# Transposes of the next expert group's rows, moved in front of the values products of their step

## The reference

```
xn  = layernorm(x)
out = x + attention(xn) + experts(xn)
attention: 16 heads of 8, causal softmax(q k^T / sqrt(8)) v, then w_proj and its bias
experts:   logits = xn Wg^T; the best 2 of 8 experts per token, gates = softmax of the two logits
           y = sum of gate * (gelu(xn W1 + b1) W2 + b2), inner size 512
```

## Time and profile before

| what | value |
|---|---|
| median of three runs (lowest, highest) | 749.66 us (740.96, 753.08) |
| the profiled execution's own time | 743.79 us |
| its span, first to last instruction | 742.0 us |
| TensorE busy, share of the span | 88% |
| VectorE, ScalarE, GpSimd busy | 71%, 59%, 37% |
| mean granted TensorE clock, share of full | 0.906 |

### The profile page before, as it was taken

How to read it: one execution, slowest core, us unless ns; L and a number is a source line. 1 busy time by engine, 2 the same in 40 slices (tenths; PEclk the granted TensorE clock), 3 DMA queues, 4 the chain that set the end, 5 groups by cost and what they waited for, 6 DMA issues and landing times.

```text
span 742.0 us, 14386 instructions
## 1 busy us (share of the span) xinstructions
PE 651.6 (88%) x4889; PEld 384.0 (52%) x4889; DVE 525.3 (71%) x1787; ACT 439.8 (59%) x652; POOL 275.2 (37%) x438
## 2 busy tenths in 40 slices
PE   5798977789893888999999999899999998999987
PEld 5554443344441546555565556556565556565533
DVE  6676677978883557668667766767777767767776
ACT  5025644536371567667576846767676757677654
POOL 5813530156776023342314322332414322333411
PEclk9556887979895799999999989999999999999979
DMA  6655572025311557144443507135443626220084
GB/s 162 196 110 158 142 200 33 20 74 192 98 58 52 161 178 192 46 123 142 128 135 97 178 19 193 61 97 172 126 139 102 175 77 186 82 83 15 29 211 129
DMA packets 95569, 88.45 MB, mean 119 GB/s; under 512 B 8560, under 2 KB 82984, under 8 KB 95496
## 3 DMA queue, kind: packets, MB, share of 16 engines
q1 hardware_dynamic: 90600, 77.21, 38.0%
q0 software_dynamic: 4544, 9.35, 3.8%
q10 hardware_dynamic: 352, 0.97, 0.5%
HBM read 49.79 MB, written 21.32 MB: 96 GB/s over the span
## 4 chain that ended last, share of the span: by engine, by line
PE 69%; DVE 15%; ACT 6%; issue 4%; DMA 3%; POOL 2%; ACTq 0%; DVEq 0%
PE ov L912 19%; PE aux L875 15%; PE aux L973 10%; DVE junk L1112 6%; PE aux L925 5%; PE sc L829 3%; PE sc L895 3%; PE aux L930 3%; ACT probs L780 2%; PE sc L830 2%; PE sc L831 2%; DVE maxes L1110 2%; POOL xs L688 2%; PE aux L953 2%; DMA qT<-mT 1%
## 5 line engine op out<-in xcount | busy, mean ns | idle before, releaser
L780 ACT ACTIVATE probs<-sc 128x1024 f32<-128x1024 f32 (+1 forms) x320 | 286.6, 941 | 168.9 <-PE sc L895 167.6
L1112 DVE CUSTOM_DVE_ANT_0 junk<-aux,cst 128x512 bf16<-128x512 f32 (+3 forms) x512 | 219.9, 487 | 39.7 <-PE aux L875 36.5
L875 PE MATMUL aux<-kT,qT 32*128 32x512 f32 (+3 forms) x768 | 201.0, 448 | 42.9 <-DVE maxes L1112 13.2
L696 POOL TENSOR_SCALAR_AFFINE_SELECT probs<-probs 128x256 f32<-128x256 f32 x224 | 89.1, 411 | 293.8 <-ACT probs L780 288.6
L1110 DVE TENSOR_REDUCE maxes<-aux 128x1 f32<-128x512 f32 x256 | 163.2, 683 | 20.6 <-PE aux L875 17.4
L912 PE MATMUL ov<-probs,v 128*32 128x512 f32 (+3 forms) x1536 | 171.1, 535 | 0.9 <-POOL probs L696 0.5
L875 PEld LDWEIGHTS aux<-kT,qT 32*128 32x128 f32 x768 | 91.2, 199 | 126.1 <-DVE maxes L1112 36.1
L895 PE MATMUL sc<-qT,kT 32*128 32x512 f32 (+3 forms) x768 | 140.7, 425 | 7.5 <-DMA qT<-mT 5.3
L711 POOL DMA_INDIRECT ys<-ysb,back x78 | 75.8, 972 | 99.7 <-DVE ysb L1160 53.9
L973 PEld LDWEIGHTS aux<-w2all,hid 128*128 128x128 f32 x624 | 77.5, 195 | 40.7 <-DVE maxes L1110 25.1
L973 PE MATMUL aux<-w2all,hid 128*128 128x128 f32 x624 | 90.0, 288 | 0.3 <-DVE kql L1049 0.3
(11 more groups left out here) (121 smaller groups left out, 582.0 us busy)
## 6 DMA issues: line engine op xcount, KB each, us to landing
w1b<-w_scr SPq DMA_DIRECT2D x39, 512.0 KB, 4.4
w2all<-in_L_ffn_W SPq DMA_DIRECT2D x39, 256.0 KB, 3.7
xs<-ysb SPq DMA_DIRECT2D x13, 387.0 KB, 5.9
kT<-kqh SPq DMA_DIRECT2D x32, 128.0 KB, 2.8
w_scr<-w1b SPq DMA_DIRECT2D x8, 512.0 KB, 4.1
qT<-kqh SPq DMA_DIRECT2D x30, 128.0 KB, 2.9
xrow<-in_L_attn_x SPq DMA_DIRECT2D x7, 512.0 KB, 5.8
xsin<-xs SPq DMA_DIRECT2D x6, 516.0 KB
```

Source lines behind the costliest of these rows:

```text
L696: last_ = nc.gpsimd.affine_select(out=block_, in_=block_, compare_op=ALU.is_ge, fill=0.0, base=0, pattern=[[0, 2], [1, P]], channel_multip ...
L780: nc.scalar.activation(probs[:, s % 2, 2 * half:2 * half + 2, 0:cols], pair(part)[:, :, 0:cols], ACT.Exp).then_inc(sc_done, 1)
L875: last_ = nc.tensor.matmul(bank(part)[:, at:at + cols], qT[n % 3][rows, P * i:P * i + P], kT[n % 3][rows, k0:k0 + cols], start=True, stop= ...
L1112: last_ = nc.vector.tensor_tensor_reduce(out=junk[:, AUXI[part] % 3, at:at + cols], in0=src, in1=cmask[:, W - cols:W], scale=1.0, scalar=L ...
```

## The change

Both `rows_in` parts of a unit, at steps 8 and 9, are appended to the list before the `values` part of the same step; before, they were appended near its end, behind `values`, the late `rows`, `send`, `down` and `load_down`. It concerns the 20 `rows_in` of units 4 to 13 (groups 1 to 10); those of group 0 stay. No instruction is added or removed.

```
--- before.py
+++ after.py
@@ -223,6 +223,8 @@
         parts.extend(x for x in group if x not in only[:4])
         if s == 0 and not f:
             late_values()
+        if nf and s in (8, 9):
+            parts.append(("rows_in", nf, s - 8))
         if s > 0:
             parts.append(("values", n, s - 1))
         parts.extend(due)
@@ -262,8 +264,6 @@
             parts.append(("load_down", f + 1))
         if nf is not None and s == (6 if nf else 8):
             parts.append(("load_rows", nf))
-        if nf and s in (8, 9):
-            parts.append(("rows_in", nf, s - 8))
```

## The result

The changed kernel takes 742.86 us (median of 22 runs, 734.78 to 752.35); the kernel before, run beside it 22 times, 746.69 us (738.04 to 754.25). The ratio is 0.9949, 95% interval 0.9928 to 0.9971: 0.5% faster, about 3.8 us (2.2 to 5.4), and far inside 2%. Over all 22 the means are 743.57 and 746.19 us, 2.6 us apart, give or take 2.5 (95%). Of the 5.4 us between forecast and measurement, 3.0 are the level: the median of before was 749.66 over three runs and is 746.69 over twenty-two.

The account below looks back on a forecast made before the run. TensorE was taken as the bound, with 69% of the chain that ended last. Six units gaining 0.34 us and four losing 0.17 gave 1.4 us, so 749.66 - 1.4 = 748.3 us; 8-in-10 range 741 to 754.

Parts of the forecast that it names:

- ScalarE's order limits the gain: Step 8, units with a `down`: two exponentials precede the cast, so 0.74 us of the transposes' 2 us move arrives.
- Unit 5, half 0: Units with a `down` in step 8, first `rows_in`: TensorE takes step 9's second adjacent `max` 0.53 us earlier.
- Half 1: Step 9's transposes newly wait for the opening `max`'s bank: 0.19 us with a `down` in step 8, 0.17 without.
- only reordered: TensorE's pieces from the released `max` to the next unit's `max`, 3.21 or 3.43 us, were taken as merely reordered.
- the net of unit 5: Each of six units with a `down` in step 8: 0.53 - 0.19 = 0.34 us gained.
- Unit 6: Each of four units without a `down` in step 8: released `max` unmoved, new bank wait in step 9 loses 0.17 us.
- Sum: All ten changed units: 6 x 0.34 - 4 x 0.17 = 1.4 us gained.
- the whole stall: Rival, step 9: TensorE's whole wait for the low part goes, 9.7 us gained, 740.0 us; chance 0.10.
- all units behave like unit 6: Rival: in all ten units only the step 9 bank wait is left, 1.7 us lost, 751.4 us; chance 0.17.
- The rows were there: Rival denied here: earlier transposes wait for the row load, 759.7 us less what is won; chance 0.03.
- The clock did not fall: Rival denied here: TensorE's clock falls once in each of ten units, 17 us less 1.4, 765.3 us; chance 0.04.
- the Trainium skill's rule on PSUM-queue cycling: Brief TensorE idling while cycling through PSUM banks lets the clock oscillate; one fall costs about 1.7 us, making a loss.

Follow-up runs that it names:

- e4_half0_between: Against the kernel before: the step 8 `rows_in` put ahead of the second scores of step 8, the step 9 one left in place; ratio 0.9965 to the kernel before.
- e1_half0_only: Against the changed kernel: only the step 8 `rows_in` stays in front of `values`, the step 9 one returns to its step's end; 0.9952 to the kernel before, 758.02 us.
- e2_half1_only: Against the changed kernel: only the step 9 `rows_in` stays in front of `values`, the step 8 one is as before; ratio 1.0069 to the kernel before.
- e3_before_again: The kernel before, with no edit, timed as one more kernel against itself; ratio 0.9992, medians 765.93 us against 760.82.
- the first four experiments: Follow-up runs timed on one chip, among them e1_half0_only and e3_before_again; the kernel before took 760.82 us there.

## Why the prediction was right, point by point

**Direction and place.** Right: slightly faster, no change by 2%, and all that the traces can compare lies in steps 8 and 9 (the table).

**ScalarE's order limits the gain.** Right and shown: of the 2 us by which the transposes moved, 0.89 us reached the cast in unit 5 (I counted 0.74). The exponentials held it back, and e4_half0_between let it go.

**Unit 5, half 0: 0.53 us gained.** Right in mechanism, too small. Half 0 alone gains 0.67 to 0.69 us in such units. The spacing from there on was right (the second `max` 0.20 us behind the first, 0.21 counted); the cast itself started 0.15 us earlier than I let it, because it overlaps the end of the exponential.

**Half 1: a wait of 0.19 us.** The wait is there, 0.21 and 0.18 us. The term was still mis-sized: half 1 in front costs 0.29 to 0.48 us a unit with the change (the change's row of the table less half 0's) and 0.29 to 0.38 alone. I had said that behind the released `max` the pieces are "only reordered", and took their sum as fixed. They are not: two transposes take 0.19 us ahead of `hidden` and 0.37 ahead of `values`. That 0.18 us is this step's failure, seen in both kernels that have the order and absent in e1_half0_only. It is no wait for a mask (e2_half1_only); what in TensorE makes it I did not test. With it, the net of unit 5 is 0.68 less 0.40, 0.28 us gained, against 0.34 forecast. That these are so near is luck in part: half 0 was counted 0.15 us too small and half 1 0.21 too small.

**Unit 6: 0.17 us lost.** Right in net (0.13 to 0.17), by two errors that cancel: half 0 gains 0.15 to 0.19 there, of which I had allowed at most 0.1 as a possibility, and half 1 costs about 0.32.

**Sum.** Forecast 1.4 us; the steps give 1.0 (6 units gain 1.6 together, 4 lose 0.6); the runs gave 3.8 (2.2 to 5.4), then 1.6 slower and 3.5 faster, with wider intervals that hold both zero and 1.0. By the ratios something stays open: 1.0 us lies outside the first interval and just outside the weighted one. Over all runs nothing does: 0.6 us, give or take 1.6. In the stretches that the traces can compare nothing else differs. So the 1.0 us of the steps is the size that the evidence bears out; that the first set of runs gained 2.8 us more is not shown to be an effect of the change.

**Rivals.** By the waits that the profile shows, the whole stall went almost as that rival said, from 10.3 to 2.3 us, and in units like 5 none is shown on the low part any more, where I had expected 0.7 or 0.8. By the starts it did not go. The `max` that opens step 9 of unit 5 in the kernel before:

```profile
327.80 0.50 PE L875 MATMUL aux<-kT,qT 32*128 32x512 f32 x1
```

From it to `values` were 1.89 us; in e1_half0_only 1.07, in e4_half0_between, where no stall is shown, 0.88. So 1.01 us of stall became 0.19. Another 0.15 us goes ahead of it: from where `values` or the transposes begin to this `max` were 2.52 us, and are 2.67. That leaves the 0.67 us that half 0 gains. In units like 6 there are 0.42 us of stall left. Half 0 alone thus won 4.7 of the 9.7 us, and half 1 gave back 3.7 of them. That all units behave like unit 6 is refuted by the table. The rows were there: in no moved place does the trace show a wait for the load, only the first group's, 12.6 us (12.3 before). The clock did not fall in these steps: the ten stretches are at 1.00 in the trace after and in those of its two repeats. The short waits, now two or three in a unit (0.33 and 0.42 us shown in unit 6, 0.15 in unit 5), did not bring down the 2.4 GHz level, so the Trainium skill's rule on PSUM-queue cycling (TensorE: Matmul & The Clock Gate, "A second HAM failure mode: psum-queue depth-cycling") did not come to bear here. The trace after has two falls that the one before has not, at 637 us (unit 13) and 678 us (unit 14). They lie outside these steps and are absent from the change's two repeats, while e3_before_again, the kernel before, has falls in the same two places.

## What to carry to other kernels

A wait of TensorE for a bank isn't always won by transposing earlier: ask what stands ahead of the *next* engine's part of the hand-over, and move only the piece whose successor waits. What stands behind the moved piece on that engine has a successor too: in e4_half0_between the stall on the low part became a wait for a mask. A part that nobody waits for, as half 1 here, is best left behind long work, because ahead of it, it meets the bank wait that the work was hiding. And where waits shrink, count from start to start: 8 us of waits less turned into 1 us of time.

## What the runs showed of the hardware

Two float32 transposes of 128x128 took 0.19 us from their start to the next piece when `hidden` products followed, 0.37 us when the values products with their 32-column weights followed; four took 0.41 and 0.59 us (the second half's in unit 6, before and after; 371.77 to 372.36 with the change). In step 8 four took 0.58 us ahead of `values` (unit 5 with the change) and ahead of scores (376.35 less 375.77 in e4_half0_between). So the short time is the one ahead of `hidden`, whose weights have the transposes' shape of 128x128. The order in which shapes of products follow one another cost nearly as much as the wait beside it.

The marks of the ten units repeat to about 0.04 us from run to run and from chip to chip, while whole runs of one program spread over 16 us. In the comparison of the first four experiments the kernel before took 760.82 us, 14 more than its 746.69. For a change of a few us the stretches at full clock tell more than a dozen timings.
